# First expert layer's combination in pairs of token tiles, and the second attention's weights, bias and first context tiles loaded and turned beside it

## The reference

```python
x = x + jnp.tanh(g_ffn[0]) * _L0_ffn_ref(_layernorm(x), ...)      # first expert layer
x = x + jnp.tanh(g_xattn[1]) * _L1_xattn_ref(_layernorm(x), ctx_2048, Wq, Wg, bg, Wkv, Wo)
x = x + jnp.tanh(g_ffn[1]) * _L1_ffn_ref(_layernorm(x), ...)      # ternary experts

# _L0_ffn_ref: 8 experts of inner width 176, two per token, and a shared one
scores = softmax(x @ gate_w.T);  topk_w, topk_idx = top_k(scores, 2);  topk_w /= sum(topk_w)
y_all = einsum('eti,eih->eth', silu(x @ w1[e]) * (x @ w3[e]), w2)
y = sum(y_all[topk_idx, tok] * topk_w[..., None], axis=1)
out = y + silu(x @ sw1) * (x @ sw3) @ sw2

# _L1_xattn_ref: linear attention, 16 heads
q = feature(query @ Wq.T);  gate = sigmoid(query @ Wg.T + bg);  k, v = split(kv @ Wkv.T)
attn = (q @ (k^T v)) / (q . sum(k) + EPS)
out = attn * gate @ Wo.T
```

## Time and profile before

| | us |
|---|---|
| median of 3 runs | 1312.31 (1310.51 to 1314.02) |
| profiled execution | 1313.03 |
| its span | 1311.2 |
| TensorE busy in it | 1015.6 (77%) |
| VectorE busy | 823.4 (63%) |
| ScalarE busy | 603.9 (46%) |
| GpSimd busy | 349.4 (27%) |
| combination, first issue to last statistic | 285.25 to 306.88 |
| first transpose of the attention's tile 0 in the chain | 315.89 |

### The profile page before, as it was taken

How to read it: one execution, slowest core, us unless ns; L and a number is a source line. 1 busy time by engine, 2 the same in 40 slices (tenths; PEclk the granted TensorE clock), 3 DMA queues, 4 the chain that set the end, 5 groups by cost and what they waited for, 6 DMA issues and landing times.

```text
span 1311.2 us, 21015 instructions
## 1 busy us (share of the span) xinstructions
PE 1015.6 (77%) x6294; PEld 766.2 (58%) x6294; DVE 823.4 (63%) x2010; ACT 603.9 (46%) x1263; POOL 349.4 (27%) x412
## 2 busy tenths in 40 slices
PE   3749189954999776778469999779999999986376
PEld 2437179953777543444335656457888888873254
DVE  7846046865666586778656566557455455476985
ACT  3454027743443375778336566533333333232474
POOL 3086604444000104665331222021111100115300
PEclk9969589985999896899679999979999999996599
DMA  6943506755200021221500000000000002100001
GB/s 203 175 131 111 184 25 208 232 177 185 68 18 6 1 74 29 65 63 53 165 9 14 13 8 1 25 24 25 25 24 24 16 8 96 64 3 15 0 17 48
DMA packets 81986, 86.33 MB, mean 66 GB/s; under 512 B 12076, under 2 KB 75327, under 8 KB 81903
## 3 DMA queue, kind: packets, MB, share of 16 engines
q1 hardware_dynamic: 75374, 68.23, 18.2%
q0 software_dynamic: 6528, 17.04, 4.0%
HBM read 60.39 MB, written 24.85 MB: 65 GB/s over the span
## 4 chain that ended last, share of the span: by engine, by line
PE 56%; DVE 14%; ACT 10%; issue 9%; POOL 4%; DMA 3%; another core or an unknown queue 2%; DVEq 1%; SPq 0%; ACTq 0%; POOLq 0%
PE bank L935 13%; PE bank L956 6%; PE bank L2925 3%; PE bank L1882 2%; PE bank L2963 2%; PE bank L2569 2%; DVE ln_stat L216 2%; PE bank L1908 2%; PE bank L2956 2%; ACT tern L2376 1%; POOL ln_rstd L242 1%; PE bank L1810 1%; DMA f_back<-f_outputs 1%; PE bank L2163 1%
## 5 line engine op out<-in xcount | busy, mean ns | idle before, releaser
L935 PE MATMUL bank<-xhi,whi 128*128 128x512 f32 x256 | 102.1, 399 | 6.0 <-PE bank L956 3.4
L935 PE MATMUL bank<-xlo,whi 128*128 128x512 f32 x256 | 101.0, 395 | 0.0
L935 PE MATMUL bank<-xhi,wlo 128*128 128x512 f32 x256 | 100.9, 394 | 0.0
L876 DVE TENSOR_TENSOR work<-work,bank 128x512 f32<-128x512 f32 x64 | 43.9, 687 | 78.6 <-PE bank L935 77.6
L854 ACT ACTIVATE ahi<-work 128x512 fp32r<-128x512 f32 x64 | 40.5, 632 | 110.3 <-DVE work L876 110.3
L822 POOL TENSOR_TENSOR wlo<-raw,whi 128x1536 fp32r<-128x1536 f32 x8 | 28.1, 3509 | 226.7 <-ACT whi L836 226.7
L956 PE MATMUL bank<-whi,ahi 128*128 128x256 f32 x256 | 73.4, 287 | 10.9 <-DVE alo L878 10.9
L851 ACT ACTIVATE work<-bank 128x512 f32<-128x512 f32 x64 | 38.2, 598 | 88.1 <-PE bank L935 87.9
L878 DVE TENSOR_TENSOR alo<-work,ahi 128x512 fp32r<-128x512 f32 x64 | 48.2, 754 | 44.7 <-ACT ahi L854 44.7
L956 PE MATMUL bank<-wlo,ahi 128*128 128x256 f32 x256 | 72.8, 285 | 0.0
L956 PE MATMUL bank<-whi,alo 128*128 128x256 f32 x256 | 72.8, 285 | 0.0
(11 more groups left out here) (513 smaller groups left out, 2997.8 us busy)
## 6 DMA issues: line engine op xcount, KB each, us to landing
f_got<-f_sorted SPq DMA_DIRECT2D x39, 129.0 KB
f_sorted<-clear_row SPq DMA_DIRECT2D x1, 4992.0 KB, 24.0
f_back<-f_outputs SPq DMA_DIRECT2D x18, 256.0 KB, 2.8
raw<-in_L_ffn_w SPq DMA_DIRECT2D x24, 176.0 KB
tern_raw<-in_L_ffn_gate_w SPq DMA_DIRECT2D x8, 512.0 KB
tern_raw<-in_L_ffn_up_w SPq DMA_DIRECT2D x8, 512.0 KB
tern_raw<-in_L_ffn_down_w SPq DMA_DIRECT2D x8, 512.0 KB
ctx_in<-in_ctx SPq DMA_DIRECT2D x32, 128.0 KB, 2.7
```

Of the source, the lines that this page charges most:

```text
L876: dve.tensor_tensor(act32[0:m, u % 2, :], silu[0:m, u % 2, :], bank[2 + u % 2][0:m, :], ALU.mult).then_inc(s.hid, 1)
L935: mm = pe.matmul(bank[2 * mat + u % 2][0:m, :], up_w(w, slot, mat, c, q), x[:, c, cols], start=j == 0, stop=j == 3 * DC - 1)
```

## The change

The combination goes by pairs of token tiles. The read of a pair is two DMAs of 256 KB, one for each choice, and `y_back` has four slots of a pair, so twice the room (it now reaches the end of `xhi` and `xlo`, which lie behind each other). GpSimd adds both tiles of a pair in one instruction of 512 columns, and so does VectorE; `s.back`, `s.pair` and `s.acc` count pairs.

SyncE issues the attention's bias row ahead of the first read, and its first four context tiles between the fourth and the fifth pair. The bias row's place moves from `mask_at`, which the expert layer still uses, to a row of `ctx_sb`. The attention's own SyncE program no longer waits for `before` and begins with the ternary loads that wait for the turned weights. TensorE's wait for `before` moves from ahead of the weight transposes to behind them.

```diff
--- before.py
+++ after.py
@@ -1432,7 +1432,7 @@
             aT_hi = over(name + "_aT_hi", xhi_at, 2048, [P, 2, DC, P], F32R)
             aT_lo = over(name + "_aT_lo", xhi_at, 2560, [P, 2, DC, P], F32R)
             y_out = over(name + "_y", xhi_at, 3072, [P, OUT_RING, D])
-            y_back = over(name + "_back", xhi_at, 4096, [P, OUT_RING, K, D])
+            y_back = over(name + "_back", xhi_at, 4096, [P, OUT_RING, K, 2, D])
             got = over(name + "_got", work_at, -2048, [P, IN_RING, ROW])
             small_area = over(name + "_places", mask_at, 0, [P, 392])
 
@@ -1537,11 +1537,15 @@
                     beside.sync(sp, j, s)
                 for j in range(NT - OUT_RING, NT):
                     sp.wait_ge(gone[j % OUT_RING], gone_up_to(j))
-                rows = g.outputs[0:K * TOK, :].rearrange("(k t p) d -> t p k d", k=K, p=P)
-                for t in range(TILES):
-                    if t >= OUT_RING:
-                        sp.wait_ge(s.acc, t - OUT_RING + 1)
-                    sp.dma_start(y_back[:, t % OUT_RING, :, :], rows[t]).then_inc(s.back[t % OUT_RING], 16)
+                beside.bias_sync(sp)
+                rows = g.outputs[0:K * TOK, :].rearrange("(k c q p) d -> c k p q d", k=K, q=2, p=P)
+                for c in range(TILES // 2):
+                    if c == OUT_RING:
+                        beside.context_sync(sp)
+                    if c >= OUT_RING:
+                        sp.wait_ge(s.acc, c - OUT_RING + 1)
+                    for k in range(K):
+                        sp.dma_start(y_back[:, c % OUT_RING, k], rows[c, k]).then_inc(s.back[c % OUT_RING], 16)
                 beside.behind_sync(sp)
 
             def gpsimd(pool):
@@ -1589,13 +1593,9 @@
                     pool.wait_ge(s.out, j + 1)
                     pool.indirect_dma_start(g.outputs, bass.IndirectOffsetOnAxis(ap=dest[:, j:j + 1], axis=0),
                                             y_out[:, j % OUT_RING, :], None).then_inc(gone[j % OUT_RING], 16)
-                for t in range(TILES):
-                    pool.wait_ge(s.back[t % OUT_RING], 16 * (t // OUT_RING + 1))
-                    for k in range(1, K):
-                        if k > 1:
-                            pool.wait_ge(s.pair, t * (K - 1) + k - 1)
-                        pool.tensor_tensor(y_back[:, t % OUT_RING, 0, :], y_back[:, t % OUT_RING, 0, :], y_back[:, t % OUT_RING, k, :],
-                                           ALU.add).then_inc(s.pair, 1)
+                for c in range(TILES // 2):
+                    pool.wait_ge(s.back[c % OUT_RING], 16 * K * (c // OUT_RING + 1))
+                    pool.tensor_tensor(two(c, 0), two(c, 0), two(c, 1), ALU.add).then_inc(s.pair, 1)
 
             def scalar_high(act, e):
                 staged(act, e)
@@ -1781,14 +1781,19 @@
                     if j + 2 < NT:
                         vector_low(dve, j + 2)
                     beside.vector(dve, j)
-                for t in range(TILES + 1):
-                    if t < TILES:
-                        dve.wait_ge(s.pair, (t + 1) * (K - 1))
-                        dve.tensor_tensor(X[:, t, :], X[:, t, :], y_back[:, t % OUT_RING, 0, :], ALU.add).then_inc(s.acc, 1)
-                    if t:
-                        dve.wait_ge(s.acc, t)
-                        next_stat(dve, t - 1)
+                for c in range(TILES // 2 + 1):
+                    if c < TILES // 2:
+                        dve.wait_ge(s.pair, c + 1)
+                        dve.tensor_tensor(flat(X[:, 2 * c:2 * c + 2, :]), flat(X[:, 2 * c:2 * c + 2, :]), two(c, 0), ALU.add).then_inc(s.acc, 1)
+                    if c:
+                        dve.wait_ge(s.acc, c)
+                        for t in (2 * c - 2, 2 * c - 1):
+                            next_stat(dve, t)
                 dve.sem_inc(done, TILES)
+
+            def two(c, k):
+
+                return flat(y_back[:, c % OUT_RING, k])
 
             def vector_shared(dve, b):
                 dve.wait_ge(p.down, (b + 1) * NC)
@@ -1960,6 +1965,8 @@
                 ternary.sync(sp, 5)
 
             beside.behind_sync = behind_sync
+            beside.bias_sync = lambda sp: layer1_weights.load_bias(sp)
+            beside.context_sync = lambda sp: layer1_weights.load_context(sp, range(RING))
             beside.behind_scalar = ternary.behind_scalar
             beside.scale = ternary.beside_scale
             steps_at = {1: ("pay", "places"), 3: ("which",), 5: ("powers",), 7: ("series",), 9: ("weights",)}
@@ -1986,7 +1993,7 @@
             den, per_den = lay(2, HEADS), lay(2, HEADS)
             attended, attendedT = lay(2, D), lay(2, D)
             raw_w = over("a1_raw_w", work_at, ternary.slot_at[1], [P, 10, D])
-            bias_row = over("a1_bias_row", mask_at, 0, [1, D])[:, :]
+            bias_row = ctx_sb[0:1, 0, :]
             head_mask = sb("a1_head_mask", [P, AUG])
             norm = make_norm(2)
             s = Names()
@@ -2003,16 +2010,21 @@
             def load_weights(sp, w):
                 name, _, a, n = weights[w]
                 sp.dma_start(raw_w[:, a:a + n, :], io[name].rearrange("(a p) k -> p a k", p=P)).then_inc(weight.loaded, 16)
-            layer1_weights.load = load_weights
-
-            def sync(sp):
-                sp.wait_ge(*before)
+
+            def load_bias(sp):
                 sp.dma_start(bias_row, io["L1_xattn_bg"].partition_broadcast(1)).then_inc(weight.loaded, 16)
-                tiles = io["ctx_2048"].rearrange("b s d -> (b s) d").rearrange("(t p) d -> t p d", p=P)
-                for t in range(TILES):
+
+            def load_context(sp, tiles):
+                for t in tiles:
                     if t >= RING:
                         sp.wait_ge(s.in_ps, t - RING + 1)
-                    sp.dma_start(ctx_in[:, t % RING, :], tiles[t]).then_inc(ctx_here[t % RING], 16)
+                    sp.dma_start(ctx_in[:, t % RING, :], io["ctx_2048"].rearrange("b s d -> (b s) d")[t * P:(t + 1) * P, :]).then_inc(ctx_here[t % RING], 16)
+            layer1_weights.load, layer1_weights.load_bias, layer1_weights.load_context = load_weights, load_bias, load_context
+
+            def sync(sp):
+                for t in range(RING - 1, TILES):
+                    if t >= RING:
+                        load_context(sp, (t,))
                     if t == RING - 1:
                         sp.wait_ge(weight.turned, was.turned + 4)
                         ternary.sync(sp, 6)
@@ -2130,7 +2142,6 @@
                 tp.then_inc(s.in_ps, 1)
 
             def tensor(pe):
-                pe.wait_ge(*before)
                 pe.wait_ge(weight.loaded, was.loaded + 16 * 5)
                 for j, (_, _, a0, n) in enumerate(weights):
                     for c in range(DC):
@@ -2139,6 +2150,7 @@
                             tp = pe.transpose(bank[j + at // 512][:, at % 512:at % 512 + P], raw_w[:, a0 + a, c * P:(c + 1) * P], ident[:, :])
                     tp.then_inc(weight.turned, 1)
                 pe.wait_ge(weight.ready, was.ready + DC * len(weights))
+                pe.wait_ge(*before)
                 pe.wait_ge(s.ones, 1)
                 ternary.tensor(pe, 4)
                 tensor_in(pe, 0, 0)
```

## The result

| | before | changed |
|---|---|---|
| median of 20 runs each, us | 1314.53 (1310.51 to 1318.06) | 1310.05 (1303.24 to 1315.81) |
| profiled execution, span | 1313.03, 1311.2 | 1310.54, 1308.6 |

The ratio is 0.9967, interval 0.9955 to 0.9979: 4.3 us or 0.33% faster (2.8 to 5.9 us); the two medians lie 4.5 us apart. The forecast was 6.6 us off and 1305.7; the time is 0.85 above the upper end of the range. Of the 4.35 us between forecast and time, 2.2 are the starting point (three runs of before had a median of 1312.31, twenty have 1314.53), and 2.1 are the change itself. From the three-run median the same gain would have ended at 1307.8, inside the range; it took both parts to put the time outside it.

What follows compares the result with a forecast made beforehand. Bound: a chain of waits between the first expert layer's last matmul and attention tile 0, no engine at its limit. 6.3 + 0.7 - 0.4 = 6.6 us off, giving 1305.7 us from the 1312.31 median; range 1302.8 to 1309.2.

Steps and rivals of the forecast that it cites:

- Weights turned early: Ahead of attention tile 0: bias, weight transposes and copies leave the path, tile 0 then waits for the norm; 6.3 us gained.
- the context tiles cost nothing at 306.6: SyncE's issuing: the context tiles' old place at 306.6 was said to cost nothing.
- Combination in pairs: End of the first expert layer: more reads in flight, fewer additions; statistics end at 306.2 instead of 306.88, 0.7 us gained.
- the first pair there after 3.85: Combination's reads: the first pair was forecast to be there at 289.1, with the first issue at 285.25.
- The fifth pair's read: SyncE's issuing in the combination: issues end at 291.2, when the first pair is added, so this read is not held back.
- the 1.9 us that I had for additions that hardly overlap: Combination's cost per pair if GpSimd's 1.30 us and VectorE's addition hardly overlap; statistics then end at 306.9.
- The second rival: Combination: additions hamper each other more, a pair costs 2.1 to 2.26 us; total gain 3.8, about 1308.5 us; chance 0.18.
- The rule of the Trainium skill: Combination: two-input SBUF VectorE instructions and GpSimd's SBUF reads block each other fully; statistics end at 306.9, gain zero.
- The clock: TensorE at attention tile 0: the rise to 2.4 GHz may come later in the work; 0.4 us lost, ends 0 and 1.5.
- Last tile moved as the first: Second attention: its last tile should move by what its first has; otherwise the prediction is wrong.

Runs made afterwards that it cites:

- e1: The kernel before with only the bias issued ahead of the reads and the weights turned early; ratio to before 0.9978.
- the repeat: The changed kernel, unaltered, measured and profiled again on one of the experiments' chips; ratio to before there 0.9976.
- e6: The changed kernel with only TensorE's wait for the layer's end put back ahead of the weight transposes; ratio to before 0.9992.
- e3: The changed kernel with the four context tiles issued behind the last pair's read instead of in the middle; ratio to before 0.9959.
- e4: As e3, but each pair is read by tile, both choices of a tile in one DMA; ratio to before 0.9972, again 0.9963.
- e7: As e4, with 16 unused filler matmuls on TensorE ahead of tile 0; ratio to before 0.9963.
- e9: From e4, TensorE instead of GpSimd sums the two choices in PSUM, with the weight turning between its pairs; ratio to before 0.9997.
- before's repeat: The kernel before, unaltered, measured and profiled again on one of the experiments' chips; ratio to before 1.0003.
- e2: The changed kernel with bias, context tiles and weight turning in their old places, so pairs only; ratio to before 0.9987.

## Why the prediction was right in its large term and wrong in the small one

- *Weights turned early, 6.3 us: right.* From last statistic to tile 0's first transpose it is 8.87 in before and 2.64 in the changed kernel, 6.2 less. The transposes began 1.25 us behind the bias's issue, not 2.75, which changed nothing. What I had at nothing, and the runs show at 2.0 us, is the early context (e1): I wrote that the context tiles cost nothing at 306.6, which was true only while the bias and the turning were later still.
- *Combination in pairs, 0.7 us gain: this step failed, and in it the landing of the second pair.* The forecast has the statistics end 20.95 us behind the first issue (306.2); they ended at 22.44, and at 22.16 in the repeat, so that 0.7 gained became 0.8 and 0.6 lost. I had the first pair there after 3.85 and the pieces land 1.5 us apart, so the second at 5.4, with 15.6 us left from there. The first was added at 3.74 (3.85 in the repeat), the second at 7.19 (6.70), and from there it took 15.3 (15.5). The second pair's lateness of 1.8 (1.3) us covers the whole miss of 1.5 (1.2). It also passes on through the slots: the sixth pair's read goes out only when VectorE has added the second pair (296.35), and lands at 301.60. Why the second pair comes so late stays open; what the runs do show is that more than its own bytes are moved before it is complete, and that neither the turning (e6), the context (e3) nor the form of the read (e4, e7) is seen to set it.
- *What was wrong inside those 15.6 us cancelled, which is luck.* The fifth pair's read, said not to be held back, was held 0.9 us by the context's issuing, which costs 0.3 to 0.9 by the distances; a pair cost less than the 1.9 us that I had for additions that hardly overlap (1.68 in e4 where the data are there).
- The second rival has the nearest number (the combination loses 1.8 us, the whole gains 3.8, 1308.5, chance 0.18; the runs show 0.8 and 4.5), but not the reason: it had each pair cost 2.1 to 2.26 because the additions hamper each other more, and from the third pair to the eighth a pair took 1.87 (295.84 to 305.19).
- The rule of the Trainium skill that I weighed (SBUF — State Buffer, section "Who interferes with whom") gave a gain of zero here. The rows above agree with it but for 0.15 us (VectorE's addition ends 0.54 behind GpSimd's, where alone it takes 0.69); in before I had read 0.12 us of the same kind, and took from it the 0.7 us by which my 306.2 is better than 306.9.
- *The clock, 0.4 us: right in this pair of profiles.* From tile 0's first transpose to its result 18.94 us in before, 19.35 in the changed kernel. In the repeats it is 18.45 and 19.35, so 0.9: there before's granted clock read 1.00 already while tile 0's first transposes ran (291.4 to 293.0), and in its first profile not before 321.2.
- *Last tile moved as the first: not quite.* The first moved 5.0, the last 4.1. The 0.9 between is the last tile's four matmuls, in the chain of the changed kernel (granted clock 0.50) and in that of before (1.00):

```profile
446.48 2.06 PE bank L2175 x4
```

```profile
449.59 1.12 PE bank L2163 x4
```

Tile 15 comes 117.0 us behind tile 0 in this profile, in e3 and in e9, and 116.0 in the other fourteen, both repeats among them, so this loss belongs to single executions and not to the change.

What stays open: the landmarks of the repeat have gained 5.2 us at tile 0's result against before's repeat, its median only 3.1 (interval 1.5 to 4.4), and over all fourteen changed kernels the medians show about 1 us less than the landmarks, with 842.1 to 847.3 us behind tile 15 for one and the same program. Whether a part is given back there or single profiles are just that uneven isn't told apart by these runs.

## What to carry to other kernels

When a loop is a round trip over a few slots, raise the number of pieces in flight first and leave the pieces small: here depth alone was worth 2.8 to 3.0 us, and larger pieces took 0.4 to 2.2 back through the second landing and 0.7 through the tail. Forecast the landing of the second of several queued reads too, and not only the first and the rate: here it waited while data from behind it were moved. Float32 additions on VectorE with both operands in SBUF beside ones on GpSimd overlapped by 0.3 to 0.4 us a couple only: 1.55 to 1.68 us at 512 columns where one after the other makes 1.95, 0.84 at 256 where it makes 1.14. Cost them nearly as if the engines were one before the work is split between them. Work whose inputs have been there for tens of us and that stands behind a general "layer done" wait was the sure gain here; and when it leaves the path, move what was hidden behind it too.

## What the runs showed of the hardware

- The granted clock read 0.99 from 292.8 to 295.9, when TensorE did nothing at all, after 20 transposes that ran from 288.40 to 292.7 at 1.2 GHz; in before the same 20 were over at 313.73 and dense work was still at 1.2 GHz until 321.2. The rise came where nothing could use it.
- 1 KB took 1.25 us from its issue to the first instruction that waits for it where the DMA engines did nothing else (287.15 to 288.40, share 0.00 to 0.01), 1.24 in e2, where the loads ahead of it ran out while it was under way, and 2.75 and 3.57 behind 1.5 MB of loads in before and its repeat.
- Four context tiles of 128 KB needed 2.24 to 2.46 us to be issued behind eight reads of 256 KB (changed kernel, its repeat, e6), and 1.77 to 1.90 where they stood elsewhere.
- TensorE's float32 pass over 512 columns takes 0.43 us at 2.4 GHz and 0.89 at 1.2 (e9), so the sum of a pair's two choices by identity, four passes, costs 1.72 us at best where VectorE's addition takes 0.69. The granted clock read 1.00 from 267.9 to 281.8 there, and the four passes of the first pair, behind 7.7 us without work, were the slow ones.
